# One core, a four-layer conditional network: transfers reissued in another order, roundings staggered, batch 7 put on the turned path

## What is computed

```
x = x + L0(x, cond)                       # base + LoRA
x = x + L1(x, cond)                       # per-batch mixed weight
# L2, for each batch b, for its top two experts e with weight w:
out += w * (gelu(x @ gate[e]) * (x @ up[e])) @ down[e]
out += (gelu(x @ sg) * (x @ su)) @ sd     # shared expert
x = x + out
# L3, one expert e per batch:
x = x + (silu(x @ Wu[e].T + bu) * (x @ Wg[e].T + bg)) @ Wd[e].T + bd
```

## Time and profile before

| what | value |
|---|---|
| three runs | 82.66, 83.45, 83.62 us |
| the profiled execution | 82.93 us, of which the span from first to last instruction is 81.5 us |
| TensorE busy | 77.0 us, 94% of the span |
| VectorE, ScalarE, GpSimd busy | 53.0 (65%), 47.0 (58%), 45.7 us (56%) |
| SyncE's queue (q1) | 20.77 MB, 71.5% of the 16 DMA engines' span |
| granted TensorE clock, mean | 1.000 |
| chain that ended last | PE 84%, DMA 6%, DVE 3%, SyncE's sequencer 2% |

### The profile page before, as it was taken

The page is one execution under the profiler, slowest core; times in us unless marked ns, Lnnn a source line. Parts: engine busy times, 40 slices in busy tenths (PEclk is TensorE's granted clock), DMA queues, the critical chain, the costliest instruction groups (busy, mean ns, idle before and its releaser), DMA issues.

```text
span 81.5 us, 1612 instructions
## 1 busy us (share of the span) xinstructions
PE 77.0 (94%) x500; PEld 69.2 (85%) x500; DVE 53.0 (65%) x116; ACT 47.0 (58%) x95; POOL 45.7 (56%) x44
## 2 busy tenths in 40 slices
PE   6999999999999999999699994999999999999990
PEld 6978998888888998988387964989989999999990
DVE  1468889869993467275896934779489374257371
ACT  6410895877587796249996395168252342168260
POOL 3001199297699999999999999993800000000000
DMA  1998000589999999999998999999999877400202
GB/s 15 329 349 348 16 0 8 102 344 332 404 411 433 416 416 411 394 423 407 382 230 281 304 385 386 321 342 330 387 415 369 277 158 216 138 0 8 63 1 64
DMA packets 8791, 21.65 MB, mean 265 GB/s; under 512 B 976, under 2 KB 5200, under 8 KB 8784
## 3 DMA queue, kind: packets, MB, share of 16 engines
q1 hardware_dynamic: 8496, 20.77, 71.5%
q10 hardware_dynamic: 288, 0.79, 2.5%
HBM read 17.88 MB, written 0.52 MB: 226 GB/s over the span
## 4 chain that ended last, share of the span: by engine, by line
PE 84%; DMA 6%; DVE 3%; SPq 2%; issue 1%
PE bank L942 16%; PE bank L915 9%; PE bank L957 9%; DMA b_mix<-p 6%; PE bank L928 4%; PE bank L926 4%; PE bank L925 4%; PE bank L878 4%; PE bank L886 4%; PE bank L894 4%; PE bank L972 4%; PE bank L809 4%; PE bank L817 3%; PE bank L902 2%; PE bank L904 2%; PE bank L901 2%
## 5 line engine op out<-in xcount | busy, mean ns | idle before, releaser
L356 POOL TENSOR_TENSOR pair_low<-pair_w,wide_h 128x512 fp32r<-128x512 f32 x16 | 20.1, 1299 | 1.5 <-ACT wide_h L449 1.5
L411 ACT ACTIVATE gelu<-bank 128x512 f32<-128x512 f32 x24 | 14.0, 594 | 10.2 <-PE bank L928 5.7
L672 DVE SCALAR_TENSOR_TENSOR hid<-gelu,wsel,bank 128x512 f32<-128x512 f32 x16 | 11.8, 736 | 7.2 <-ACT gelu L411 2.0
L361 POOL TENSOR_TENSOR hid_l<-hid,hid_h 128x512 fp32r<-128x512 f32 x8 | 10.2, 1292 | 2.8 <-ACT hid_h L467 2.8
L925 PE MATMUL bank<-wide_h,x_h 128*128 128x512 f32 x24 | 10.0, 417 | 0.8 <-DVE hid L672 0.8
L421 ACT ACTIVATE half<-bank,half_bias 128x128 f32<-128x128 f32 x12 | 3.7, 363 | 11.0 <-PE bank L957 6.5
L449 ACT ACTIVATE wide_h<-pair_w 128x512 fp32r<-128x512 f32 x16 | 9.1, 623 | 1.3 <-DMA pair_w<-in_skill 1.3
L686 DVE STREAM_TRANSPOSE p<-hid 128x512 f32<-128x512 f32 x12 | 8.5, 711 | 2.1 <-DMA b_mix<-p 1.2
L926 PE MATMUL bank<-wide_h,x_l 128*128 128x512 f32 x24 | 9.4, 391 | 0.0
L915 PE MATMUL bank<-x_t,pair_w 128*128 128x128 f32 x64 | 7.5, 275 | 0.0
L915 PEld LDWEIGHTS bank<-x_t,pair_w 128*128 128x128 f32 x64 | 7.4, 192 | 0.1
(11 more groups left out here) (114 smaller groups left out, 159.4 us busy)
## 6 DMA issues: line engine op xcount, KB each, us to landing
pair_w<-in_skill SPq DMA_DIRECT2D x12, 768.0 KB, 7.2
w<-in_layer SPq DMA_DIRECT2D x6, 384.0 KB, 7.9
x_t<-p SPq DMA_DIRECT2D x12, 128.0 KB, 3.8
b_mix<-p SPq DMA_DIRECT2D x12, 128.0 KB, 5.6
shared_sb<-in_skill SPq DMA_DIRECT2D x1, 768.0 KB, 12.3
home_h<-in_skill SPq DMA_DIRECT2D x1, 768.0 KB, 6.9
home_l<-in_skill SPq DMA_DIRECT2D x1, 768.0 KB, 8.2
home_hid<-in_skill SPq DMA_DIRECT2D x1, 768.0 KB, 9.6
```

What stands on the lines that cost most here:

```text
L356: pool.tensor_tensor(low_of(b, k)[:, m, :], w[:, m, :], wide_h[:, ring_at(b, k) % RING, m, :].bitcast(fp32), ALU.subtract).then_inc(wide_l ...
L361: pool.tensor_tensor(hid_l[:, k % 3, :], hid[:, k % 2, :], hid_h[:, k % 3, :].bitcast(fp32), ALU.subtract).then_inc(hid_low, 1)
L411: act.activation(gelu[:, n, :], ps[:, :], ACT.Gelu_apprx_tanh).then_inc(gelu_ready, 1)
L672: dve.scalar_tensor_tensor(hid[:, n, :], gelu[:, n, :], wsel[:, bass.DynSlice(weight, 1)], u_ps[n][:, :], ALU.mult, ALU.mult).then_inc(hid ...
```

## The change

Four things are changed. `TURNED` becomes `range(1, B)`, so batch 7 goes the turned way too. SyncE's list is rewritten. ScalarE's roundings are put one pair at a time between the gelus rather than one batch at a time (the helpers `round_batch` and `gelus` go). VectorE does `hidden` and `turn` of (2,0) ahead of `layer3(0)`, and near the end `residual(6)` ahead of `gated3(5)`. TensorE's list has batch 7 in the common loop, and the last steps are in another order.

```diff
-TURNED = range(1, B - 1)
+TURNED = range(1, B)
...
-                load_w3(0, picked[0, 0])
                 for b, k in ((2, 0), (2, 1), (3, 0)):
                     pick(b, k)
                     load(b, k)
+                load_w3(0, picked[0, 0])
...
-                load_w3(1, picked[1, 0])
-                load_w3(2, picked[2, 0])
...
                 sp.wait_ge(down_done, down_at(0, 0))
                 load(5, 1)
+                load_w3(1, picked[1, 0])
+                swap(2)
                 sp.wait_ge(down_done, down_at(0, 1))
                 load(6, 0)
-                swap(2)
-                load_w3(3, picked[3, 0])
-                store(0, 0)
                 swap(3)
                 sp.wait_ge(down_done, down_at(1, 0))
                 load(6, 1)
-                load_w3(4, picked[4, 0])
+                load_w3(2, picked[2, 0])
+                swap(4)
                 sp.wait_ge(down_done, down_at(1, 1))
                 load(7, 0)
-                swap(4)
                 sp.wait_ge(down_done, down_at(2, 0))
                 load(7, 1)
+                load_w3(3, picked[3, 0])
+                store(0, 0)
+                swap(5)
+                load_w3(4, picked[4, 0])
+                store(1, 1)
                 load_w3(5, picked[5, 0], 1)
-                swap(5)
+                swap(6)
                 load_w3(6, picked[6, 0], 2)
-                store(1, 1)
-                swap(6)
+                store(2, 0)
                 load_w3(7, picked[7, 0], 3)
+                swap(7)
...
-                round_batch(2)
-                gelus(1)
-                round_batch(3)
+                round_pair(2, 0)
+                round_pair(2, 1)
+                expert_gelu(1, 0)
+                round_pair(3, 0)
+                expert_gelu(1, 1)
+                round_pair(3, 1)
+                expert_gelu(2, 0)
                 halve3(0)
                 tanh_step(0)
...
+                expert_gelu(6, 0)
+                round_pair(7, 0)
+                expert_gelu(6, 1)
+                round_pair(7, 1)
...
+                expert_hidden(2, 0)
                 layer3(0)
-                expert_hidden(2, 0)
...
+                residual(B - 2)
                 gated3(B - 3)
-                residual(B - 2)
...
-                gate_up(B - 1, 0)
-                gate_up(B - 1, 1)
-                down3(B - 5, 1)
-                down(B - 3, 0)
-                down(B - 3, 1)
-                layer3(B - 4)
                 down(B - 2, 0)
+                down(B - 2, 1)
                 layer3(B - 3)
-                down(B - 2, 1)
                 down3(B - 4, 0)
+                product3(B - 2, 0, 0, 0)
                 down(B - 1, 0)
                 down3(B - 3, 1)
-                product3(B - 2, 0, 0, 0)
                 down(B - 1, 1)
```

More of the change, by code:

```diff
@@ L308, in _ @@
                 load(6, 1)
-                load_w3(4, picked[4, 0])
+                load_w3(2, picked[2, 0])
+                swap(4)
                 sp.wait_ge(down_done, down_at(1, 1))
                 load(7, 0)
-                swap(4)
                 sp.wait_ge(down_done, down_at(2, 0))
                 load(7, 1)
+                load_w3(3, picked[3, 0])
[3 more added lines that the diff above has]
+                store(1, 1)
                 load_w3(5, picked[5, 0], 1)
-                swap(5)
+                swap(6)
                 load_w3(6, picked[6, 0], 2)
-                store(1, 1)
-                swap(6)
+                store(2, 0)
                 load_w3(7, picked[7, 0], 3)
-                for b in range(2, B - 2):
+                swap(7)
+                for b in range(3, B - 2):
                     store(b, b % 2)
@@ L453, in round_pair, with expert_gelu @@
                         round_part(b, k, m)
[L455 to L461, removed]
+                def expert_gelu(b, k):
+                    gelu_step(NSH + TOP_K * b + k, k, g_ps[k])
                 def round_hidden(k):
@@ L475, in _ @@
                 round_hidden(NSH - 1)
-                gelu_step(NSH, 0, g_ps[0])
+                expert_gelu(0, 0)
                 round_pair(1, 1)
-                gelu_step(NSH + 1, 1, g_ps[1])
-                round_batch(2)
-                gelus(1)
-                round_batch(3)
+                expert_gelu(0, 1)
+                round_pair(2, 0)
[5 more added lines that the diff above has]
+                expert_gelu(2, 0)
                 halve3(0)
                 tanh_step(0)
[L484 to L488, removed]
+                expert_gelu(2, 1)
+                round_pair(4, 0)
+                expert_gelu(3, 0)
+                round_pair(4, 1)
+                expert_gelu(3, 1)
+                round_pair(5, 0)
+                expert_gelu(4, 0)
+                round_pair(5, 1)
+                expert_gelu(4, 1)
                 round_pair(6, 0)
@@ L491, in _ @@
                 tanh_step(1)
[L492 to L497, removed]
+                expert_gelu(5, 0)
+                expert_gelu(5, 1)
+                round_pair(6, 1)
+                halve3(2)
+                tanh_step(2)
+                expert_gelu(6, 0)
+                round_pair(7, 0)
+                expert_gelu(6, 1)
+                round_pair(7, 1)
+                halve3(3)
+                tanh_step(3)
+                expert_gelu(7, 0)
+                expert_gelu(7, 1)
+                halve3(4)
+                tanh_step(4)
                 halve3(B - 3)
@@ L1021, in _ @@
                 layer3(1)
-                for b in range(5, B - 1):
+                for b in range(5, B):
                     gate_up_wide(b, 0)
```

## The result

The changed kernel is slower. Its median is 84.61 us (84.04 to 85.19, 4 runs) against 83.16 us before (82.66 to 83.62, 4 runs): a ratio of 1.022, 95% interval 1.0162 to 1.0278. Run again later (experiment 8) it came to 1.0184 (1.0078 to 1.029). The forecast was 81.3, range 80.2 to 82.6, so the time lies 2.0 above the range's upper end.

What follows compares the result with a forecast made beforehand. TensorE, busy 94%, was taken as the bound, losing time in few gaps or its own work. Terms -0.74 - 0.1 - 1.23 - 0.73 + 0.9 = -1.9 gave 81.0 or 81.55 us; forecast 81.3, range 80.2 to 82.6.

Steps and rivals of the forecast that it cites:

- VectorE's order: Hidden of (2,0) done ahead of layer3(0) lets pair (3,1) start at about 41.87, not 42.61: 0.74 us gained.
- the wide form of batch 7: TensorE's gate and up of batch 7 take 2.84 us where the other form took 3.57: 0.73 gained.
- its swap: Down(7,0) waits for the new swap of batch 7; the turned batch costs 0.9 us there, range 0.6 to 1.3.
- The rival in which this swap is hidden: The swap of batch 7 is nearly hidden, 0.9 less: 80.4 us, at best 80.2; chance 0.13.
- the 59.7 from which I said it would cost: Pair (7,0) landing after 59.7 us costs its excess, since TensorE wants GpSimd's result at 65.3.
- Two of the signs of being wrong: Listed: waits for pair_low or wide_high in batches 4 or 7, layer3(1), (2) or (3) awaiting weights, batch 2's swap after 48.
- SyncE's order: Fewer transfers ahead bring the swaps of batches 1 and 2 sooner; down(1) gains 0.1 us and down(2) 1.23.
- the count: DMA queue landings priced in issue order: 2.0 us per pair, 1.5 per swap, 1.0 per layer 3 weight.
- the layer 3 weights of batch 3 "at nothing", with a cover of 0.7: They land at 61.1, layer3(3) is due at 61.8: no cost, 0.4 us at the bad end.
- The queue is fuller than I count: Rival: 0.4 us more behind each of three swaps; 0.5 to 1.3 given back, 81.8 to 82.6; chance 0.26.
- The waits only change place: Rival: VectorE's chain of hidden, turn and layer3 fills the room, 83.0 to 83.5 us; no gain had chance 0.07.
- The chance of slower, 0.04: Rival: pair (7,0) lands late, its load behind the swaps of batches 3 and 4: 85.3 us or more; chance 0.04.

Runs made afterwards that it cites:

- experiment 8: The changed kernel itself, nothing edited, timed again beside the kernel before and experiments 5 to 7 on one chip: ratio 1.0184.
- experiment 4: The kernel before with VectorE's order alone (hidden and turn of (2,0) ahead of layer3(0)): ratio 0.9986.
- experiment 7: The changed kernel with batch 3's layer 3 weights issued right behind batch 2's, ahead of the swap of batch 4 and batch 7's pairs: ratio 1.0212.
- experiment 12: The kernel of experiment 11 with load(5,1) issued ahead of the swap of batch 1: ratio 1.0281.
- experiment 1: The changed kernel with the layer 3 weights of batches 1 and 2 issued early again, behind pair (3,1): ratio 1.0028.
- experiment 3: The changed kernel with SyncE's list of the kernel before and swap(7) at its end: ratio 1.0078.
- experiment 5: The kernel before with VectorE's and ScalarE's new order, without batch 7's turn: ratio 1.0046.
- experiment 15: The kernel of experiment 13 without early routing or batch 7's turn, batch 3's layer 3 weights right behind (6,1): ratio 0.9968.
- experiment 6: The changed kernel with load(6,0) ahead of the swap of batch 2 and load(7,0) ahead of the swap of batch 4: ratio 1.0324.
- experiment 11: The kernel of experiment 1 with the early routing of experiment 10 on top: ratio 1.0104.
- experiment 10: The kernel before with routing ready sooner: VectorE, not GpSimd, writes the table of chosen experts right after the ranking: ratio 1.0045.
- experiment 13: The kernel of experiment 11 with halve3(1) and tanh_step(1) ahead of the rounding of (6,0) on ScalarE: ratio 0.9963.
- experiment 2: The changed kernel without batch 7's turn (no swap(7), no roundings of its pairs): ratio 1.0091.

## Why the prediction was wrong

**Right: VectorE's order.** 0.63 of 0.74 was gained, with hidden at the times worked out. It needs ScalarE's new order too: with VectorE's alone (experiment 4) the gelu is late. **Right: the wide form of batch 7**, 0.75 for 0.73, and **its swap**, 0.82 for 0.9 (0.94 lost at down(7,0), 0.12 won behind it): issued 70.8 to 72.6, landed 75.4, as by the row of the swap of batch 6. The rival in which this swap is hidden is out. Pair (7,0) landed at 60.6 where I had 58.2, past the 59.7 from which I said it would cost; it cost nothing because TensorE came to batch 7 at 65.4, where I had 62.7. Experiment 7, where it comes at 64.2 and (7,0) lands at 61.7, has that wait.

Two of the signs of being wrong that the prediction names came: the swap of batch 2 landed after 48, and layer3(3) waited for its weights.

**Wrong: "SyncE's order", the step "For the swap of batch 2 one layer 3 weight and one pair are gone: 50.1 - 1.0 - 2.0 = 47.1".** It takes the landings as one sum: remove something ahead, and all behind moves up by its price. The lead was there at first: (4,0) landed at 36.9 for 38.9 and (5,0) at 40.9 for 42.7. The swap of batch 1 kept 0.6 of it (43.6 for 44.2), since it was issued from 38.0 to 40.0 in both kernels, and (5,1) kept none: 46.8 for 46.6, where the count had 44.6. Pair (5,1) is issued at 41.6, behind the last part of that swap, whose issue alone took 1.41 us; it lands 5.2 later.

In the sixteen profiled runs other than experiment 12 it was issued between 40.7 and 42.5 and landed between 45.8 and 47.3. In six of them (the kernel before and experiments 1, 3, 4, 5, 15) pair (5,0) had landed at 42.7 to 43.4, on average 43.0, and (5,1) lands at 46.7 on average: by the count, 43.0 + 1.5 + 2.0 = 46.5. In the other ten (5,0) had landed at 40.7 to 41.9, on average 41.2, and (5,1) lands at 46.7 all the same, where the count has 44.7; that is 4.8 behind its issue. In experiment 12, issued at 34.1, it landed at 44.2: by the count 40.9 + 2.0 and 1.1 for the three parts that landed before it, 44.0. So the count holds while issues run ahead of the queue, and fails where they don't. It also takes landings to come in the order of issue, which the last section shows to be only roughly so. Behind the pair the prices held: 1.0 for the weights of batch 1, 1.5 for the swap, so 49.3. I had put a floor of issue plus 5.0 under the swaps and left it off the pair between them. With the 40.8 + 5.8 of the earlier trace rows kept for the pair, 46.6 + 1.0 + 1.5 = 49.1 could have been had from the rows.

**Wrong: the layer 3 weights of batch 3 "at nothing", with a cover of 0.7.** They landed at 64.5, the count had 61.1. Of the 3.4, 2.2 are the same step ((5,1) at 46.8, not 44.6). The other 1.2 lie between (5,1) and the weights: by the kernel before, four pairs, three swaps and three weights take 62.1 - 46.6 + 1.0 = 16.5 (its stretch from (5,1) to (7,1), and one weight more); here they took 64.5 - 46.8 = 17.7. A pair steps 2.1 to 2.9 behind the landing ahead, where I used 2.0. Layer3(3) was due at 64.57 - 1.23 = 63.34, so without this 1.2 its weights would just have been in time. What the 1.2 comes from stays open. The loads stand behind the swaps now, and (6,0) is issued at 45.9 (42.1 before) and (7,0) at 54.2 (51.4), but experiment 6, with both loads ahead of the swaps again, needs 64.6 - 46.8 = 17.8. Experiments 1 and 11 need 17.4 with two weights fewer in the stretch. And with SyncE's list of before, in which (5,1) to (7,1) took 15.5, the same stretch takes 14.9 in experiment 10, 16.2 in 3, 17.2 in 4 and 17.4 in 5: from run to run the count over ten transfers scatters by up to 2.5, and the cover was 0.7. I had seen that SyncE's waits are in series, and weighed it only for (7,0). That the weights' new place is what makes them late is shown: experiment 3, with SyncE's old list, has them at 51.1 and no such wait, and experiment 7 has them at 58.4.

**Missed: a late pair on ScalarE.** Pair (6,0), 3.6 later than before, was in time for TensorE's own use, but `halve3(1)` queues behind its rounding; experiments 11 and 13 show the link, 0.25 here and 1.41 there.

**The rivals.** "The queue is fuller than I count" had the right direction and the wrong size: it put 0.4 behind each swap, 0.5 for batch 3's weights, and ended at 82.6. "The waits only change place" stopped at 83.0 to 83.5; experiments 3 to 5 (83.78, 82.80, 83.42) are near that case. In 3 and 5 the reason is one I had not given, the swaps; in 4 it is the one given, layer 3 and the gelus on ScalarE and VectorE. No rival let a transfer that moved from 51.0 to 64.5 decide. The chance of slower, 0.04, rested on (7,0) alone; the weights of batch 3, with 0.7 of cover under a count over ten transfers, were the nearer danger.

The terms of the table give the span's +1.0. The median moved by 1.45; the rest is time outside the span and scatter between runs (spans of 82.0 to 83.5 in four runs of the changed kernel), and no run here divides it.

## What to carry over

In these runs a landing was close to the later of two times: that of the transfer ahead plus its own step (2.0 us for a pair), and its own issue plus its time in a queue that has run low (4.4 to 5.2 us for a pair). Both must be priced for every transfer, most of all after something was taken out ahead. A sum over many transfers must be held against how far it scatters between runs before a cover is called enough. In a list that is issued in order, a wait in front of a load delays all behind it, and a transfer moved later needs its new landing held against its user, and against what stands behind that user on its engine. When several waits lie close behind one another, curing one shows the next, so the cover of each must be listed before one is priced as a gain.

## What the hardware showed

A pair of 768 KB (pair (5,1)) landed 4.4 to 5.2 us after an issue near 41.6 to 42.1 where the queue had run low (experiments 2, 6, 10, 11 and the changed kernel). Landings are not strictly in order of issue: in the changed kernel the first two parts of the swap of batch 3 were issued after pair (6,0) and landed at 51.4 and 51.9, the pair at 52.2, the fourth part at 53.6.

SyncE's issue instructions are not of one price. In the changed kernel a load of a pair took 0.33 to 0.46 us, most parts of a swap 0.55 to 0.68, and near 40 to 42 us one instruction took 0.9 to 1.6 whatever it was: the pair in the kernel before (1.16) and in experiment 1 (0.94), the fourth part of the swap in the changed kernel (1.41) and in experiment 10 (1.55). In these four it ended between 41.4 and 42.3. Only in experiment 12, where (5,1) had been issued at 34.1, is there no such instruction (the longest part took 0.73). What holds SyncE there is open. Open too is why a pair in the stretch from 46 to 63 us steps 2.1 in one place and 2.9 in another. Late issue does not explain it by itself: in experiment 6, with (6,0) and (7,0) issued sooner, the pairs step 1.9 to 3.1.
